# A rebuilt setup and other instruction orders in an eight-batch attention and expert block

## What is computed

```python
mod = (silu(c) @ wmod).reshape(8, 6, 1, -1)          # sa, ca, ga, sb, cb, gb
h = layernorm(x) * (1 + ca) + sa
x = x + ga * attention(h)      # 16 heads, 64 rotary + 16 content columns a head
h = layernorm(x) * (1 + cb) + sb
x = x + gb * experts(h)        # 8 chosen experts, SwiGLU, top-8 weights
```

## Time and profile before

| what | us |
|---|---|
| median of 3 runs (1019.28 to 1020.67) | 1019.88 |
| the profiled execution | 1020.3 |
| its span, first to last instruction | 1018.6 |
| PE busy in the span | 962.8 (95%) |
| DVE, POOL, ACT busy | 685.2, 496.8, 426.2 |
| setup, until the first score | 67.2 |
| batch periods (store to store), batches 1 to 6 | 118.4, 117.2, 118.6, 117.1, 118.9, 118.0 |
| from batch 6's store to the end | 121.1 |

### The profile page before, as it was taken

One profiled execution on the slowest core, in us unless ns is written; L12 is line 12 of the kernel. 1 busy time (PEld: TensorE's weight loads), 2 busy tenths in 40 slices (PEclk: granted clock), 3 DMA queues, 4 the chain that ended last, 5 costly groups with the idle time before them and its releaser, 6 DMA issues.

```text
span 1018.6 us, 23971 instructions
## 1 busy us (share of the span) xinstructions
PE 962.8 (95%) x9847; PEld 704.9 (69%) x9847; DVE 685.2 (67%) x1371; ACT 426.2 (42%) x780; POOL 496.8 (49%) x462
## 2 busy tenths in 40 slices
PE   5789999999999999999999999999999999998897
PEld 3546667766687677866777667866778667875566
DVE  5676767675776757667676758777576766766334
ACT  5234444264433634344442644245443445333332
POOL 2345454673545552663625644555526636356202
PEclk9889999999999999999999999999999999999999
DMA  6322010210102101200102101030002101011000
GB/s 205 81 87 84 33 62 2 75 63 2 63 1 95 43 11 53 73 33 33 63 2 73 64 2 63 7 99 33 33 33 73 49 17 63 1 53 64 2 1 21
DMA packets 37599, 48.73 MB, mean 48 GB/s; under 512 B 9386, under 2 KB 23210, under 8 KB 37490
## 3 DMA queue, kind: packets, MB, share of 16 engines
q1 hardware_dynamic: 37490, 47.20, 13.9%
HBM read 17.80 MB, written 4.21 MB: 22 GB/s over the span
## 4 chain that ended last, share of the span: by engine, by line
PE 75%; DVE 9%; ACT 6%; POOL 4%; issue 3%; DMA 2%; SPq 2%; POOLq 0%; DVEq 0%; ACTq 0%
PE ring L1206 15%; PE ring L1053 11%; PE ring L1054 9%; PE ring L1055 9%; PE ring L1178 7%; PE av L1222 7%; ACT pt L746 3%; DVE mcol L943 3%; PE ring L1283 2%; PE ring L1285 2%; PE ring L1284 2%; DVE prod L919 2%; PE ring L1190 2%; PE ring L1114 1%; SPq L537 1%
## 5 line engine op out<-in xcount | busy, mean ns | idle before, releaser
L746 ACT ACTIVATE pt<-ring 128x384 f32<-128x384 f32 (+1 forms) x384 | 171.0, 533 | 256.7 <-PE ring L1206 226.8
L943 DVE TENSOR_REDUCE mcol<-ring 128x1 f32<-128x128 f32 (+3 forms) x512 | 211.1, 482 | 47.8 <-PE ring L1183 47.2
L624 POOL TENSOR_SCALAR_AFFINE_SELECT pt<-pt 128x512 f32<-128x512 f32 x128 | 81.0, 646 | 215.4 <-ACT pt L746 215.4
L919 DVE TENSOR_TENSOR prod<-ring,table 128x1024 f32<-128x1024 f32 x128 | 154.5, 1217 | 44.4 <-PE ring L1055 40.1
L1206 PE MATMUL ring<-rows 32*128 32x512 f32 (+3 forms) x3072 | 172.2, 329 | 6.5 <-ACT pt L746 5.3
L1206 PEld LDWEIGHTS ring<-rows 32*128 32x128 f32 x3072 | 127.4, 184 | 53.4 <-issue 20.4
L597 POOL TENSOR_TENSOR rows<-prod,rows 128x1024 fp32r<-128x1024 f32 x64 | 152.6, 2390 | 17.3 <-ACT rows L725 16.4
L590 POOL TENSOR_TENSOR prod<-prod 128x512 f32<-128x512 f32 x64 | 82.0, 1281 | 87.2 <-DVE prod L919 86.6
L1178 PE MATMUL ring<-rows 32*128 32x512 f32 (+3 forms) x1024 | 89.9, 361 | 16.3 <-DMA cont<-h_lo 4.7
L725 ACT ACTIVATE rows<-prod 128x1024 fp32r<-128x1024 f32 x64 | 67.7, 1073 | 88.0 <-POOL prod L591 83.1
L1222 PE MATMUL av<-pt,vals 128*17 128x512 f32 (+3 forms) x1024 | 87.3, 447 | 4.3 <-POOL pt L624 4.3
(11 more groups left out here) (189 smaller groups left out, 1798.5 us busy)
## 6 DMA issues: line engine op xcount, KB each, us to landing
cont<-h_hi SPq DMA_DIRECT2D x96, 128.0 KB, 2.0
cont<-h_lo SPq DMA_DIRECT2D x96, 128.0 KB, 2.0
xn<-x_dram SPq DMA_DIRECT2D x8, 512.0 KB, 4.7
xr<-x_dram SPq DMA_DIRECT2D x8, 512.0 KB, 4.2
out_dram<-xr SPq DMA_DIRECT2D x8, 512.0 KB, 3.2
gate_bc<-gates_scratch SPq DMA_DIRECT2D x8, 256.0 KB, 4.4
pt<-wmod_dram SPq DMA_DIRECT2D x1, 1536.0 KB, 6.7
pt<-gup_t_dram SPq DMA_DIRECT2D x16, 96.0 KB, 2.5
```

The lines of the kernel that those rows point to most:

```text
L746: sc.activation(pt[:, PT_AT[n] + h * w:PT_AT[n] + (h + 1) * w], ps[:, 0:w], ACT.Exp, scale=SCALE).then_inc(exp_ready.sem, 1)
L919: ve.tensor_tensor(prod[:, s % PROD, :, :], ps[:, :].unsqueeze(1).broadcast_to([P, 2, S]), table[:, :, :], ALU.mult).then_inc(rotated.sem, 1)
L943: last = ve.reduce_max(mcol[:, q, h * HR + ONE_ROW:h * HR + ONE_ROW + 1], ps[:, at:at + (q + 1) * P], AX_X)
```

## The change

**Setup.** The x load goes ahead of the modulation weights, which are loaded in two parts (first the two used by the first norm). The rotary key weights are loaded and split in two parts (head group 0, then the rest; the rest's lo part goes to POOL as `split_kl`). Tables come before the small weights. Memsets go from DVE to POOL, behind the mask; the mask copies get a step (`masks`) ahead of the first norm; `consts` follows on DVE. `mod` becomes two steps; `mod.1`, `gates` and the second half of the gates' arithmetic (`gates2`) go behind the first products, and the gates' buffer from `xr` to `xn`. Two `heat` steps run 16 and 6 matmuls of the identity with itself. `split_k` of head group 0 follows `fuse.0`, and the `fuse` pieces get another order, with waits `CON_FUSED` and `ROPE_FUSED`. All four first moves (`move_k.00`, `.01`, `move_q.00`, `.01`) stand on SP in front of the expert loads, now the step `load_gu`. `split_ffn.1` goes to POOL; both `split_ffn` stand at setup's end. `spread` goes into batch 0's body.

**Body.** The same steps in another order: `maxima.010` first, `qcon.01` behind `shift.01`, `stats1.1` ahead of `rotate.0210`, `value.012`, `turn1.10`, `turn1.11` and `shift.02` in a row with `score.020` right behind, `maxima.102` ahead of the experts, `values.11` at the end, `hi.111` among the experts, `loads.0` between the moves.

**Last part.** The same steps in another order: rope, qcon and kcon spread between scores and maxima; `warm.00` goes from before the last values to behind `mix.01`, so that `warm.00` and `warm.02` stand in a row; `top` ahead of most gates, `weigh.00` earlier.

```diff
-FUSE = [(c, at, min(512, NQ - at)) for at in (0, NG * NROPE, 512) for c in range(EC)]
+FUSE = [(c, at, min(512, NQ - at)) for at, c in ((0, 0), (NG * NROPE, 0), (NG * NROPE, 1), (0, 1), (512, 0), (512, 1))]
+CON_FUSED, ROPE_FUSED = 3, 4
+HEAT = [16, 6]
...
 SETUP_ORDER = """
-latent.0 latent_hi.0 latent_lo.0 fuse.1 rope.0000 rotate.0000 rope.0001 rotate.0001 combine.000 kcon.00 kcon_hi.00 kcon_lo.00 move_k.00 rope.0010 rotate.0010 rope.0011 rotate.0011 hi.000 lo.000 combine.001 fuse.2 fuse.3 hi.001 lo.001 rope.0100 rotate.0100 qcon.00 qcon_hi.00 qcon_lo.00 move_q.00 rope.0101 rotate.0101 combine.010 values.00 values_out.00 values.01 values_out.01 move_k.01 hi.010 maxima.000 reduce.000 lo.010 rope.0110 rotate.0110 maxima.001 reduce.001 rope.0111 rotate.0111 combine.011 maxima.002 reduce.002 fuse.4 fuse.5 move_q.01 shift.00 shifted.00 hi.011 lo.011 spread. split_ffn.0 split_ffn.1 load_late.
+latent.0 latent_hi.0 latent_lo.0 rope.0000 rotate.0000 split_uv. rope.0001 rotate.0001 combine.000 split_kh. kcon.00
+kcon_hi.00 kcon_lo.00 move_k.00 move_k.01 mod.1 gates. fuse.1 hi.000 fuse.2 fuse.3 split_kl. qcon.00
+qcon_hi.00 qcon_lo.00 move_q.00 move_q.01 load_gu. rope.0010 rotate.0010 rope.0011 rotate.0011 combine.001 hi.001 lo.000
+gates2. rope.0100 rotate.0100 rope.0101 rotate.0101 values.00 values_out.00 values.01 values_out.01 lo.001 combine.010
+maxima.000 reduce.000 hi.010 rope.0110 rotate.0110 maxima.001 reduce.001 rope.0111 rotate.0111 combine.011
+maxima.002 reduce.002 lo.010 fuse.4 fuse.5 shift.00 shifted.00 hi.011 split_ffn.0 lo.011 split_ffn.1 load_late.
 """
 BODY_ORDER = """
-rope.0200 score.000 rotate.0200 load_next.1 rope.0201 exp.000 loads.0 maxima.010 rotate.0201 clear.000 qcon.01
...
-pow1.1 value.010 exp.011 maxima.020 combine.030 norm1.1 rope.0311 reduce.020 score.012 clear.011 rotate.0311
-maxima.021 combine.031 exp.012 move_q.03 maxima.022 hi.030 move_k.03 reduce.021 hi.031 clear.012 turn1.10 reduce.022
-turn1.11 lo.030 modulate1.10 value.011 modulate1.11 low1.10 shift.02 maxima.030 shifted.02 low1.11 value.012
-reduce.030 score.020 attn_out.01 score.021 exp.020 maxima.031 clear.020 exp.021 value.020 reduce.031 clear.021 lo.031
...
+maxima.010 rope.0200 reduce.010 load_next.1 score.000 rotate.0200 rope.0201 exp.000 score.001 rotate.0201 spread.
+stats1.1 combine.020 rope.0210 exp.001 maxima.011 rotate.0210 clear.000 rope.0211 reduce.011 pow1.1 maxima.012
+rotate.0211 clear.001 value.000 reduce.012 combine.021 value.001 score.002 shift.01 exp.002 kcon.01 shifted.01 qcon.01
...
+maxima.022 norm1.1 loads.0 move_q.03 rotate.0311 clear.012 value.011 reduce.022 combine.031 value.012 hi.030 turn1.10
+turn1.11 modulate1.10 shift.02 lo.030 shifted.02 modulate1.11 low1.10 score.020 hi.031 low1.11 attn_out.01 maxima.030
...
 LAST_ORDER = """
...
+value.022 score.031 exp.030 attn_out.02 clear.030 exp.031 wofold.0 value.030 score.032 clear.031 value.031 exp.032
+warm.01 clear.032 value.032 attn_out.03 mix.00 mix.01 mixed.00 warm.00 mixed.01 warm.02 stats2.0 pow2.0 norm2.0
...
 def setup_steps():
-    out = [("silu",), ("stats1", 0), ("pow1", 0), ("norm1", 0), ("mod",), ("split_d",), ("split_k",), ("turn1", 0, 0), ("turn1", 0, 1),
-           ("gates",), ("modulate1", 0, 0), ("low1", 0, 0), ("modulate1", 0, 1), ("low1", 0, 1), ("fuse", 0), ("split_uv",)]
+    out = [("heat", 0), ("silu",), ("stats1", 0), ("masks",), ("split_d",), ("pow1", 0), ("norm1", 0), ("mod", 0), ("consts",),
+           ("turn1", 0, 0), ("turn1", 0, 1), ("modulate1", 0, 0), ("low1", 0, 0), ("modulate1", 0, 1), ("low1", 0, 1),
+           ("heat", 1), ("fuse", 0), ("split_k", 0)]
...
-            sp.dma_start(ct[:, :, :], c_t.rearrange("(c p) b -> p c b", p=P)).then_inc(ld_mod, 16)
-            sp.dma_start(wmod_st, wmod.rearrange("(c p) n -> p c n", p=P)).then_inc(ld_mod, 16)
+            wmod_src = wmod.rearrange("(c p) n -> p c n", p=P)
+            sp.dma_start(ct[:, :, :], c_t.rearrange("(c p) b -> p c b", p=P)).then_inc(ld_c, 16)
             sp.dma_start(xn[:, :, :], x_rows(0, 0)).then_inc(x_loaded.sem, 16)
+            sp.dma_start(wmod_st[:, :, 0:2 * E], wmod_src[:, :, 0:2 * E]).then_inc(ld_mod, 16)
...
+                    elif kind == "load_gu":
+                        sp.wait_ge(mod_read, 2)
+                        sp.wait_ge(gates_read, 1)
...
+            pool.memset(wuk_l0[:, :].bitcast(F32), 0.0)
+            pool.memset(wuv_l0[:, :].bitcast(F32), 0.0)
+            for part_of in (1, 3):
+                pool.memset(cont[:, :, part_of, :].bitcast(F32), 0.0)
+            pool.memset(spread[:, :].bitcast(F32), 0.0)
+            pool.memset(wT[:, :].bitcast(F32), 0.0).then_inc(pool_setup, 1)
...
+                    if kind == "heat":
+                        pe.wait_ge(consts_ready, 1)
+                        ps = take_bank(pe, b, part, step)
+                        for _ in range(HEAT[step[1]]):
+                            last = pe.matmul(ps[:, 0:P], ident[:, :], ident[:, :], start=True, stop=True)
+                        last.then_inc(full_sem, 1)
...
-                            pe.wait_ge(fuse_read, EC)
+                            pe.wait_ge(fuse_read, ROPE_FUSED)
+                        elif part == "setup" and half == 0:
+                            if g == 0:
+                                pe.wait_ge(keys_split, 2)
+                            else:
+                                pe.wait_ge(keys_lo_rest, 1)
```

More of the change, by code:

```diff
@@ L94 @@
[L94 to L98, removed]
@@ new lines @@
+clear.002 score.010 qcon_hi.01 kcon_hi.01 qcon_lo.01 hi.020 kcon_lo.01 move_q.02 value.002 lo.020 rope.0300 move_k.02
+exp.010 score.011 rotate.0300 hi.021 clear.010 attn_out.00 lo.021 rope.0301 exp.011 maxima.020 rotate.0301 clear.011
+value.010 reduce.020 combine.030 maxima.021 rope.0310 reduce.021 score.012 rotate.0310 rope.0311 exp.012 move_k.03
+maxima.022 norm1.1 loads.0 move_q.03 rotate.0311 clear.012 value.011 reduce.022 combine.031 value.012 hi.030 turn1.10
+turn1.11 modulate1.10 shift.02 lo.030 shifted.02 modulate1.11 low1.10 score.020 hi.031 low1.11 attn_out.01 maxima.030
@@ new lines @@
+exp.020 score.021 reduce.030 clear.020 wofold.0 maxima.031 lo.031 exp.021 value.020 reduce.031 clear.021 maxima.032
+value.021 reduce.032 score.022 shift.03 exp.022 rope.1000 shifted.03 clear.022 score.030 rotate.1000 value.022
+rope.1001 exp.030 attn_out.02 score.031 rotate.1001 clear.030 combine.100 value.030 exp.031 score.032 hi.100 clear.031
+latent.1 exp.032 qcon.10 latent_hi.1 clear.032 latent_lo.1 value.031 lo.100 qcon_hi.10 value.032 qcon_lo.10 kcon.10
+move_q.10 attn_out.03 rope.1010 kcon_hi.10 rope.1011 rotate.1010 mix.00 rotate.1011 kcon_lo.10 combine.101 mix.01
@@ new lines @@
+mixed.00 move_k.10 rope.1100 move_q.11 mixed.01 hi.101 rope.1101 move_k.11 stats2.0 rotate.1100 pow2.0 values.10
+maxima.100 rotate.1101 values_out.10 norm2.0 maxima.101 reduce.100 combine.110 turn2.00 turn2.01 reduce.101
+modulate2.00 rope.1110 lo.101 modulate2.01 rope.1111 low2.00 low2.01 maxima.102 rotate.1110 logits.0 rotate.1111
+reduce.102 gate.00 combine.111 logits_copy.0 turn_l.0 tanh.00 gate.01 gated.00 top.0 ex.0 gate.02 tanh.01 top2.0 up.00
+tanh.02 gate.03 upped.00 gated.01 turn_w.0 up.01 wT.0 hi.110 wT_lo.0 gate.04 gated.02 tanh.03 gated.03 weigh.00
@@ new lines @@
+maxima.010 qcon.01 reduce.010 score.000 qcon_hi.01 qcon_lo.01 rope.0200 exp.000 score.001 rotate.0200 clear.000
+value.000 exp.001 maxima.011 clear.001 rope.0201 reduce.011 maxima.012 rotate.0201 rope.0210 reduce.012 combine.020
+kcon.01 rope.0211 kcon_hi.01 rotate.0210 score.002 rotate.0211 kcon_lo.01 combine.021 shift.01 exp.002 move_q.02
+value.001 shifted.01 score.010 hi.020 move_k.02 clear.002 hi.021 lo.020 value.002 exp.010 attn_out.00 maxima.020
+rope.0300 reduce.020 clear.010 lo.021 score.011 rotate.0300 value.010 exp.011 maxima.021 clear.011 rope.0301
@@ new lines @@
+reduce.021 score.012 rotate.0301 value.011 exp.012 move_q.03 maxima.022 move_k.03 rope.0310 clear.012 reduce.022
+combine.030 loads.0 rope.0311 rotate.0310 shift.02 value.012 shifted.02 hi.030 rotate.0311 score.020 attn_out.01
+combine.031 score.021 exp.020 hi.031 clear.020 lo.030 exp.021 maxima.030 value.020 reduce.030 lo.031 maxima.031
+maxima.032 reduce.031 clear.021 value.021 reduce.032 score.022 shift.03 exp.022 shifted.03 score.030 clear.022
+value.022 score.031 exp.030 attn_out.02 clear.030 exp.031 wofold.0 value.030 score.032 clear.031 value.031 exp.032
@@ L404, in last_use @@
                 prev, shift = ORDER["body"][back], -1
-            if prev is not None and prev[0] == "warm":
+            if prev is not None and prev[0] in ("warm", "heat"):
                 return None
@@ L853, in program @@
                                                 ALU.add, ALU.mult).then_inc(gates_ready, 1)
[L854 removed]
+                    elif kind == "spread" and b == 0:
                         ve.wait_ge(ld_small, 16 * N_SMALL)
@@ L875, in program @@
                         last.then_inc(fuse_read, 1)
```

(2 more changed lines are left out.)

156 lines of the change are left out of this document (88 added, 68 removed).

## The result

The changed kernel is a little slower: median 1023.89 us of 15 executions (1020.35 to 1034.67) beside 1019.98 of the kernel before, a ratio of 1.006 with a 95% interval of 1.0035 to 1.0085. A second set gave 1024.80 beside 1019.11, 1.0068 (1.0042 to 1.0094). The forecast was 1009.4.

What follows compares the result with a forecast made beforehand. PE, the busiest engine, bounds the kernel, with room in setup and the last part, little in the body. Setup 4, body 3.5 and last part 3 sum to 10.5 us off the profiled 1020.3: 1009.8, median 1009.4, range 1000 to 1019.

Steps and rivals of the forecast that it cites:

- Setup, head: Setup up to the first maxima: x lands earlier, lo part done at 17.2, last `fuse` piece read near 60; 6.5 us won.
- Setup's new small matmuls: Setup, after the first norm: `mod.1` 3.5 us and the gates 2.7 come onto PE's path, within 9.6 us given back.
- The new wait for x: Setup's tail, batch 0: x issued at 70 holds DVE at `stats1.1`, PE waits 4 to 5 us at `maxima.012`; still 4 won.
- POOL's expert split: Setup's end: `split_ffn.1` on POOL takes 3.6 us, done near 67, its wait covered by the wait for x.
- Heat: Setup's start: `heat.0` is worth nothing, as the granted clock is 1.00 when the first matmuls run.
- Body: Body batches: walk gives 1.0 us won each, half taken, 0.5; seven batches give 3.5, from 10 won to 7 lost.
- the vanished maxima hold: Body's first half: 1.6 us at held maxima goes, as `rope` and `value` steps stand between the pieces; sum 1.0 won.
- Last part: Last part: clears ahead of combines, 26 filler matmuls in a row and earlier `weigh` steps win 3 us, from 0 to 6.
- (b): Rival: only setup counts, body's hold is replaced, last part even; 4 to 5 less, 1015.5; chance 0.24 together with (c).
- (c): Rival: the clock falls in every batch from `turn1`; 4.2 on the forecast, 1013.6; chance 0.24 together with (b).
- (d): Rival: slower; bare `shift.02` to `score.020` chain costs 0.9 a batch, low clock in all seven; 1026; chance 0.10.
- (e): Rival: late x and a low clock eat setup's gain, body and last part even; 1019 to 1021; chance 0.07.

Runs made afterwards that it cites:

- the low one: Profiled execution of the changed kernel with the one-off `down` split moved early, behind `combine.111`; that kernel's median 1021.19 us, 1.0028 of before.
- the filler alone: Changed kernel plus only `heat.2`, six identity matmuls in PE's stop ahead of `kcon.00`: 1024.53 us, 1.0053 of before.
- the same edit with the old body list: `heat.2` added to new setup and last part with the body list of before: 1016.17 us, again 1016.38; 0.9971 and 0.9974 of before.
- the two unedited sets: Changed kernel without any further edit, measured twice against the kernel before: 1023.89 us (1.0060) and 1024.80 us (1.0068).
- the unedited setup: New setup without `heat.2` or moved `mod.1`; with the changed body 1023.89 and 1024.80 us, with the old body 1021.05 and 1019.11 us.

## Why the prediction was wrong, step by step

- **Setup, head: right in the profiled execution.** The lo part at 17.1 (17.2), the move's wait gone, POOL's `lo.000` as what is late next, the last `fuse` piece read at 61.4 (60). Shown by the traces, and by the exchange of `lo.000` and `combine.001`.
- **Setup's new small matmuls: mis-sized.** The step put `mod.1` and the gates at 3.5 and 2.7, their times of before; in the profiled execution they took 1.85 and 1.89, in the low one above 2.47 and 3.58. What it had at nothing is the clock behind them, and it counted 2 us won for a fall left out. They stand behind two stops of 1.36 and 1.05 us on PE's path, in 31 of 73 executions the mean clock was low, and in the three of these that were profiled it fell there, for up to 8.5 us. Of the median's miss this is 0.8 us, of the mean's 3.1.
- **The new wait for x: the time right, the cause not.** x was issued at 70.6 (70) and landed 4.1 later, at 74.7, but DVE reached `stats1.1` at 75.0 by itself: PE stopped 1.09 and 1.59 and ran `score.000` at half clock around 67 to 70, and DVE's expert split took 2.69. So no DVE idle ended by a DMA, and no stop of 4 to 5 us at `maxima.012`; that the end of `score.002` came out the same is luck.
- **POOL's expert split: covered in this kernel, but mis-sized**, 4.59 us for 3.6.
- **Heat: right in its sum, wrong in its reason.** I took the earlier trace rows, clock 1.00, as proof that the array is at full speed from the start. Without heat the 16 matmuls of `mod.0` take 3.56 us at a recorded 1.00, behind heat 1.85; the 32 in 6.99 of the earlier trace rows had that slow rate already. So heat saves `mod.0` 1.7 us, half of the 3.5 that the prediction put on it. The Trainium skill's rule (TensorE: Matmul & The Clock Gate, part 1, that the array begins at the lower clock) is borne out by that; the record of the granted clock does not show it. The time is hidden ahead of the transposes at 12.5.
- **Body: the failed term of the profiled execution.** The forecast was 0.5 won a batch. Batch 2 from its first PE instruction to `maxima.031` takes 47.17 us against 46.52, the rest 70.20 against 70.71: 0.14 lost. The 0.9 before `score.020` was right. The 1.0 won by the vanished maxima hold was not: up to `shift.02` 0.2 is won, and from there to `maxima.031` 0.8 is lost. The walk looked at `rope` and `value` steps between maxima pieces and not at the banks, and behind `score.020` three steps of four banks each follow one another. That the banks are what brings the hold back is read from the waits; no run parts these steps alone. The mean period, 118.3, is outside the 117 to 118 that the forecast set itself.
- **Batch 0's one-off work: left out.** The split of the `down` weights has no term in the sum. It cost 2.6 us of PE's time in the trace and 2.7 to 3.6 by experiment. With the 0.8 us around `score.020` it is most of the 4.0 that the first stretch lacks; the six periods lack 4.75 (from -3.0 to +1.75), the last part 1.8: together the profiled execution's 10.5.
- **Last part: 3 forecast, 0 measured.** Fillers and clears did what was said; a gap at the mix took their place.
- **Rivals.** (b) had the body and the last part right (the hold replaced, the last part even), but kept setup's 4 to 5, which batch 0 gave back. (c) looked for a fall in every batch, at `turn1`; it came in two of the six periods in place of four, twice as long, and in setup. (d) had the right sign by a place that costs little: the bare chain is there, with 0.14 a batch net in place of 0.9. (e)'s 1019 to 1021 holds the profiled execution; the median lies between (e) and (d).

What stays open: why the filler alone does not lower the changed kernel's median (1024.5) although it leaves none of its executions low, while the same edit with the old body list wins 2.7 to 4.9 us. Its six spans have a mean of 1022.2, against 1024.0 and 1024.5 of the two unedited sets and 1020.9 and 1021.6 of their executions that are not low; so a part of the gain is there, and six are few. No profile caught one of the longer ones. How exactly stop and small matmuls bring the fall together is not settled either, only that without one of them it is not seen with the old body list.

## What to carry to other kernels

When small matmuls move onto PE's path behind a stop, price what runs behind them at the lower clock too, and look at several executions: one profile can be of the lucky group. Here even the better group's median lay 2.7 us above the profiled execution. Walk a loop's first pass by itself, since its one-off splits meet another order than the later passes do. A hold on a PSUM bank that an order takes away is gone only if the next steps that take four banks each have been counted through.

## What the runs showed of the hardware

- The same 32 matmuls from the same start took 5.20 to 6.46 us, and in the unedited setup that start went with the clock 25 us later. The Trainium skill (TensorE: Matmul & The Clock Gate, part 1) says that the gate's watch runs freely and does not begin anew with a kernel, so that the point of change varies; these runs agree.
- Two splits of 1536 columns that overlapped took longer on both engines: 4.59 us on POOL, where a like one beside other work of DVE took 3.53 (L671), and 2.69 on DVE, where two in a row took 3.41 in the kernel before. No run parts the overlap from the rest.
